# Mixture of experts on one core: experts in the order of their counts, with columns fixed by rank

## The reference, cut to what matters

```python
probs = softmax(xt @ gate_w); top_p, top_i = top_k(probs, 2)      # 8 experts
for k in range(2):
    e, w = top_i[:, k], top_p[:, k]
    pos = position of the token among those whose k-th choice is e
    keep = pos < 160                                              # cap
    buf[e, pos] = xt * keep
    h = gelu(buf @ w1[e] + b1[e])                                 # 256 -> 1024
    y = h @ w2[e] + b2[e] + gelu(buf @ wd[e]) @ wu[e]
    out += y[e, pos] * keep * w
sh = gelu(xt @ sw1 + sb1) @ sw2 + sb2 + gelu(xt @ swd) @ swu
out = x + out + 0.2 * sh
```

## Time and profile before

| | us |
|---|---|
| median of 3 runs | 205.83 (204.18 to 205.94) |
| the profiled execution | 205.79 |
| its span, first to last instruction | 203.8 |
| PE busy | 193.6 (95%) |
| DVE busy | 142.3 (70%) |
| ACT busy | 132.6 (65%) |
| POOL busy | 110.5 (54%) |
| mean granted clock of PE | 0.987 |

### The profile page before, as it was taken

The page is one execution under the profiler, slowest core; times in us unless marked ns, Lnnn a source line. Parts: engine busy times, 40 slices in busy tenths (PEclk is TensorE's granted clock), DMA queues, the critical chain, the costliest instruction groups (busy, mean ns, idle before and its releaser), DMA issues.

```text
span 203.8 us, 4011 instructions
## 1 busy us (share of the span) xinstructions
PE 193.6 (95%) x1457; PEld 185.7 (91%) x1457; DVE 142.3 (70%) x308; ACT 132.6 (65%) x282; POOL 110.5 (54%) x131
## 2 busy tenths in 40 slices
PE   6999999998999999999999999999999999999960
PEld 6987779996789999999999999999999999999950
DVE  4498598859284214777897897888888887988210
ACT  2366899604295109959959959959959959949100
POOL 5400031499570251412896896886886835817471
PEclk9999999999699999999999999999999999999998
DMA  5591845307427022045858858858868765701432
GB/s 164 166 322 53 248 168 157 118 0 228 141 82 222 0 66 103 29 133 178 201 114 275 192 131 259 188 149 263 161 169 252 149 198 184 130 8 15 54 37 34
DMA packets 23816, 29.24 MB, mean 143 GB/s; under 512 B 4442, under 2 KB 20564, under 8 KB 23796
## 3 DMA queue, kind: packets, MB, share of 16 engines
q1 hardware_dynamic: 19412, 23.03, 35.5%
q0 software_dynamic: 4016, 5.38, 16.4%
q10 hardware_dynamic: 368, 0.56, 0.9%
HBM read 23.92 MB, written 5.05 MB: 142 GB/s over the span
## 4 chain that ended last, share of the span: by engine, by line
PE 75%; POOL 8%; DMA 4%; issue 4%; DVE 4%; ACT 1%; POOLq 1%; SPq 0%; DVEq 0%
PE hid_ps L826 12%; PE hid_ps L827 11%; PE hid_ps L828 11%; PE y_ps L828 9%; PE y_ps L826 9%; PE y_ps L827 9%; POOL at_place L398 6%; DMA gate_raw<-in_L_ffn_gate_w 3%; PE turn_ps L991 3%; DMA out_rows<-y_row,slot_tok 2%; POOL out_rows L384 2%; PE row_ps L1007 1%; PE hid_ps L847 1%; DVE gelu_f L601 1%; PE y_ps L953 1%
## 5 line engine op out<-in xcount | busy, mean ns | idle before, releaser
L597 DVE TENSOR_TENSOR hid_l<-gelu_f,hid_h 128x320 fp32r<-128x320 f32 (+1 forms) x80 | 42.0, 533 | 22.3 <-ACT hid_h L504 21.8
L384 POOL DMA_INDIRECT out_rows<-y_row,slot_tok x24 | 43.5, 1813 | 17.3 <-DVE y_row L750 8.9
L503 ACT ACTIVATE gelu_f<-hid_ps,bias_t 128x320 f32<-128x320 f32 (+1 forms) x77 | 44.4, 577 | 9.2 <-PE hid_ps L828 8.7
L504 ACT ACTIVATE hid_h<-hid_ps,bias_t 128x320 fp32r<-128x320 f32 (+1 forms) x77 | 44.6, 580 | 0.0
L370 POOL DMA_INDIRECT slot_in<-slot_rows,slot_src x24 | 26.7, 1111 | 22.7 <-PE turn_ps L991 15.4
L826 PE MATMUL hid_ps<-xs_h,w_h 128*128 128x288 f32 x128 | 38.2, 298 | 0.0
L828 PE MATMUL hid_ps<-xs_h,w_l 128*128 128x288 f32 x128 | 37.7, 294 | 0.0
L827 PE MATMUL hid_ps<-xs_l,w_h 128*128 128x288 f32 x128 | 37.6, 294 | 0.0
L828 PE MATMUL y_ps<-hid_h,w_l 128*128 128x288 f32 x112 | 32.9, 294 | 0.0
L827 PE MATMUL y_ps<-hid_l,w_h 128*128 128x288 f32 x112 | 32.9, 294 | 0.0
L826 PE MATMUL y_ps<-hid_h,w_h 128*128 128x288 f32 x112 | 32.9, 294 | 0.0
(11 more groups left out here) (189 smaller groups left out, 407.8 us busy)
## 6 DMA issues: line engine op xcount, KB each, us to landing
w_raw<-in_L_ffn_w SPq DMA_DIRECT2D x16, 1024.0 KB
x_in<-in_x SPq DMA_DIRECT2D x2, 512.0 KB, 4.5
w_raw<-in_L_ffn_sw SPq DMA_DIRECT2D x1, 1024.0 KB
slot_rows<-token_row SPq DMA_DIRECT2D x2, 512.0 KB, 4.2
out_rows<-base SPq DMA_DIRECT2D x2, 512.0 KB, 3.0
wu_raw<-in_L_ffn_wu SPq DMA_DIRECT2D x24, 32.0 KB
w_raw<-in_L_ffn_sw ACTq DMA_DIRECT2D x1, 512.0 KB
w_raw<-in_L_ffn_sw SPq DMA_DIRECT2D x1, 512.0 KB, 5.3
```

Of the source, the lines that this page charges most:

```text
L384: pool.indirect_dma_start(out=out, out_offset=bass.IndirectOffsetOnAxis(ap=slot_tok[0:n, e, s:s + 1].bitcast(U32), axis=0), in_=y_row[0:n, ...
L503: act.activation(gelu_f[:, j % 3, 0:n], src[:, 0:n], ACT.Gelu, bias=bias(j - 1))
L504: act.activation(hid_h[:, j - 1, 0:n], src[:, 0:n], ACT.Gelu, bias=bias(j - 1)).then_inc(hid_gelu, 1)
L597: dve.tensor_tensor(hid_l[:, j - 1, 0:n], gelu_f[:, j % 3, 0:n], hid_h[:, j - 1, 0:n].bitcast(F32), ALU.subtract).then_inc(hid_split, 1)
```

## The change

- DVE's tables are keyed by an expert's rank (the order of falling used slots, ties by number) instead of its number. So slots, gathers and scatters of "expert r" are those of the r-th fullest.
- The ranks are worked out on POOL (`rank_experts`: 14 small steps that each wait for the one before, then a copy to `order` and two scalings to `steps_down`). The counts come by an ACT copy behind gelu tile 4 of the first half, and `count_before` goes from behind hidden tile 6 to behind tile 4.
- SP reads the expert's number from `order` into a register ahead of each load of weights; the first load of an expert's w1 waits for `order`. DVE sorts the biases by rank (`sort_biases`, two passes over 512 columns).
- PE's sizes are 288, 288, 272, 272, 256, 256, 256, 256 for ranks 0 to 7, if each used count fits; else 320 for all. `turn_slots` turns only the tiles that the next expert's size needs. `last_out` leaves out the third tile when the size is 256, but for one product with 64 rows that fills its bank (POOL and DVE still weigh and scatter it), and the third tile comes first.
- `map_slots` goes from behind hidden tile 1 of the second half to behind tile 5; `side_data` from split 1 to split 5.
- wd and wu of the first expert go on POOL behind at_place, on DVE behind split 6; the first expert's w2 chunks go on DVE behind the shared rows, on ACT behind the gelus of the second half.
- In the last expert `weigh_rows(6)` comes ahead of all splits, and the four w2 chunks come behind splits 1 to 4 (all four, where three came in the period before).
- The scatters have no bounds check.

```diff
+STEP = P // 8
+COUNT_AT = 4
+STEPS_AT = (2, 4)
+SIZES = [FEW - STEP * sum(r >= s for s in STEPS_AT) for r in range(E)]
...
+        last_tiles = [ST - 1] + list(range(ST - 1))
...
             def load_first(v):
-                e = v - 1
+                if v == 1:
+                    sp.wait_ge(order_known, 1)
+                at_rank[v] = sp.value_load(order[0:1, v - 1:v], min_val=0, max_val=E - 1)
+                e = at_rank[v]
                 sp.wait_ge(w1_lo, v * CHUNKS)
...
-                        in_=y_row[0:n, s, :], in_offset=None, bounds_check=T + SLOTS - 1,
+                        in_=y_row[0:n, s, :], in_offset=None,
                         compute_op=ALU.add).then_inc(combined, 16)
...
             wd_hi_part(0, 0)
             wu_hi_part(0, 0)
-            wd_hi_part(1, 1)
-            wu_hi_part(1, 1)
...
+            def rank(ins):
+                ranks[0] += 1
+                ins.then_inc(ranking, 1)
+                pool.wait_ge(ranking, ranks[0])
+
+            def rank_experts():
+                pool.wait_ge(used_copied, 1)
+                pool.wait_ge(consts, 11)
+                rank(pool.tensor_scalar(count16[:, :, :], used_raw[:, :, :], float(CAP), float(E), ALU.min, ALU.mult))
+                rank(pool.tensor_tensor(tie[:, :], count16[:, 0, :], count16[:, 1, :], ALU.add))
+                rank(pool.tensor_tensor(tie[:, :], tie[:, :], col_of[:, 0, :], ALU.subtract))
+                rank(pool.tensor_tensor(is_more[:, :, :], tie[:, :].unsqueeze(1).to_broadcast([P, E, E]),
+                                        tie[:, :].unsqueeze(2).to_broadcast([P, E, E]), ALU.subtract))
...
+                pool.tensor_copy(order[:, :], tie[:, :]).then_inc(order_known, 1)
+                for i, s in enumerate(STEPS_AT):
+                    ins = pool.tensor_scalar(steps_down[:, i, :], rank_at[:, :], float(s), float(STEP), ALU.is_ge, ALU.mult)
+                ins.then_inc(rank_ready, 1)
...
             for j in range(HT):
                 gelu_tile(0, j, HALF, shared_bias)
+                if j == COUNT_AT:
+                    act.wait_ge(pos_made, 1)
+                    act.activation(used_raw[:, :, :], turn_ps[0][:, NT * K * E:(NT + 1) * K * E].rearrange(
+                        "p (k e) -> p k e", k=K), ACT.Copy).then_inc(used_copied, 1)
             for c in range(CHUNKS):
                 w1_chunk(1, 1, c)
+            for j in range(HT):
+                gelu_tile(1, j, HALF, shared_bias)
             for c in range(CHUNKS):
                 w2_chunk(1, 1, c)
-            for j in range(HT):
-                gelu_tile(1, j, HALF, shared_bias)
...
             def key_tokens():
 
+                dve.wait_ge(rank_ready, 1)
+                step(dve.tensor_tensor(picked[:, :, :, :], chosen[:, :, :, :],
+                                       rank_at[:, :].unsqueeze(1).unsqueeze(1).to_broadcast([P, NT, K, E]), ALU.mult))
+                step(dve.tensor_reduce(rank_tok[:, :, :], picked[:, :, :, :], AX_X, ALU.add))
...
-            wd_part(1, 1)
-            wu_part(1, 1)
             for j in range(HT):
                 split_tile(1, j, HALF)
-                if 1 <= j <= CHUNKS:
-                    w2_chunk(j - 1, 1, 1)
-                if j == 1:
+                if j == 5:
                     side_data()
+                if j == 6:
+                    wd_part(1, 1)
+                    wu_part(1, 1)
             for t in range(HTILES, NT):
                 shared_row(t)
+                if t == HTILES:
+                    w2_chunk(0, 1, 1)
+                    w2_chunk(1, 1, 1)
                 if t == HTILES + 1:
                     slots_lo_part(0)
+                if t == HTILES + 2:
+                    sort_biases()
+            w2_chunk(2, 1, 1)
+            w2_chunk(3, 1, 1)
 
             def period(e, par, rows=True, split=True):
 
+                if e == E - 1:
+                    weigh_rows(e - 1, 1 - par)
...
-                    for c in range(CHUNKS - LATE_LO):
+                    for c in range(CHUNKS - LATE_LO if e + 2 < E else 0):
...
-                    if h == 0 and j == HT - 3:
+                    if h == 0 and j == COUNT_AT:
                         count_before()
-                    if h == 1 and j == 1:
+                    if h == 1 and j == 5:
                         map_slots()
...
             with pe.If(most <= FEW):
-                experts(FEW)
+                experts(SIZES)
             with pe.Else():
-                experts(SLOTS)
+                experts([SLOTS] * E)
```

More of the change, by code:

```diff
@@ L189, in build @@
         places_known = sem("places_known")
+        ranking = sem("ranking")
+        used_copied = sem("used_copied")
+        order_known = sem("order_known")
+        rank_ready = sem("rank_ready")
+        bias_picked = sem("bias_picked")
+        bias_sorted = sem("bias_sorted")
         keyed_made = sem("keyed_made")
@@ L711, in value_tokens, with sort_biases @@
                 step(dve.tensor_tensor(used_by[:, :], used[:, 0, :], used[:, 1, :], ALU.add))
+                for i in range(len(STEPS_AT)):
+                    step(dve.tensor_tensor(used_by[:, :], used_by[:, :], steps_down[:, i, :], ALU.add))
                 dve.tensor_reduce(most_used[:, :], used_by[:, :], AX_X, ALU.max).then_inc(used_known, 1)
+            def sort_biases():
+                picks = y_t[:, :, :].rearrange("p k n -> p (k n)")[:, 0:E * NF * E].rearrange("p (r f e) -> p r f e", r=E, f=NF)
+                dve.tensor_tensor(picks, bias_t[:, 0:N_BIAS1].rearrange("p (e f) -> p f e", e=E).unsqueeze(1).to_broadcast(
+                    [P, E, NF, E]), has_rank[:, :, :].unsqueeze(2).to_broadcast([P, E, NF, E]), ALU.mult).then_inc(bias_picked, 1)
+                dve.wait_ge(bias_picked, 1)
+                dve.tensor_reduce(bias_s[:, :, :], picks, AX_X, ALU.add).then_inc(bias_sorted, 1)
             def side_data():
@@ L756, in weigh_last @@
                 dve.wait_ge(slots_sided, 1)
-                for s in range(ST):
+                for i, s in enumerate(last_tiles):
                     n = ST_ROWS[s]
-                    dve.wait_ge(y_made, y_before(e + 2) + (s + 1))
+                    dve.wait_ge(y_made, y_before(e + 2) + (i + 1))
                     dve.tensor_scalar(y_row[0:n, s, :], last_bank[s][0:n, 0:D], slot_w[0:n, e, s:s + 1], None,
@@ L966, in last_out @@
                 pe.wait_ge(y_weighted, e * ST)
-                for s in range(ST):
+                pe.wait_ge(hid_split, hid_count(e + 2, 0))
+                tiles = [s for s in last_tiles if size > s * P]
+                if ST - 1 not in tiles:
+                    pe.matmul(last_bank[ST - 1][0:ST_ROWS[ST - 1], 0:D], low_s[:, (ST - 1) * P:SLOTS], wu_s[par][:, :],
+                              start=True, stop=True).then_inc(y_made, 1)
+                for s in tiles:
                     n = min(P, size - s * P)
@@ L979, in last_out, with turn_slots @@
                     ins.then_inc(y_made, 1)
-            def turn_slots(e, par):
+            def turn_slots(e, par, tiles):
                 pe.wait_ge(slots_in[par], (e // 2 + 1) * 16 * ST)
                 if e == 0:
-                    pe.wait_ge(consts, 9)
+                    pe.wait_ge(consts, 11)
                     pe.wait_ge(slots_sided, 1)
@@ L989, in turn_slots @@
                 for k in range(KD):
-                    for s in range(ST):
+                    for s in range(tiles):
                         ins = pe.transpose(turn_ps[k][:, s * P:(s + 1) * P], slot_in[par][:, s, k * P:(k + 1) * P],
@@ L1036, in _, with experts @@
                     if h == 1 and t == 1:
-                        turn_slots(0, 0)
-            def experts(size):
-                for e in range(E):
+                        turn_slots(0, 0, ST)
+            def experts(sizes):
+                for e, size in enumerate(sizes):
                     other = (e + 1) % 2
@@ L1048, in experts @@
                     if e < E - 1:
-                        turn_slots(e + 1, other)
+                        turn_slots(e + 1, other, (sizes[e + 1] + P - 1) // P)
                         for m in range(KD):
```

62 lines of the change are left out of this document (49 added, 13 removed).

## The result

The median after is 198.57 us (197.73 to 199.96, four runs), against 205.88 us for the kernel before in the same job: a ratio of 0.966, interval 0.960 to 0.973. The change makes the kernel 7.3 us faster; 11.1 us were forecast. 198.57 lies just above the predicted range.

A forecast was written before the change was run, and what follows sets the result against it. PE was taken to bound the expert loop, busy 95% of the span. Shorter experts 5.75, less 0.1 for small waits, map and clock 3.5, end 1.9: 11.05 us off 205.79, giving 194.7 us, range 192.2 to 198.2.

The forecast's parts named there:

- the steps: POOL's rank chain: 0.9 us each for four steps to 34 us, 0.45 after; order at 38.7, no cost forecast.
- The map: PE's map products, moved later in the second half, would take 1.75 us instead of 3.53: 1.8 us saved.
- The clock's part: Eight hidden products behind the map would take 1.8 us instead of 3.5 at full clock: 1.7 us saved.
- SP's reading of the register: SP reading the expert's number ahead of the first w1 load: 0.5 us, between 0 and 1.5.
- the first load: Load of the first expert's w1, issued behind the order: 5.8 us, so the order may come at 39.8.
- It just fits: POOL's loop of about 13.5 us fits PE's 13.6 us period in the short experts; 0.1 us added for small waits.
- rival (b): Short experts: POOL or DVE binds at 14.2 us for a 13.6 period, taking back 2.4 us: 197.1; chance 0.12.
- The pace terms: PE's expert products: 272 columns save 0.0058 us each, 256 save 0.0117; with fewer transposes, 5.75 us before H.
- H: Begin of the last expert's hidden products, 180.1 us in the profile before; times at the end count from it.
- The chain of scatters: POOL's scatters carry the end: third scatter at H+16.25, end at H+21.8 instead of H+23.7, 1.9 us saved.
- The third tile that `last_out` leaves out: Last expert's third output tile, 2.9 us of PE, hidden behind the scatter chain: costs and gives nothing.
- The bounds check: Removing it from scatters saves 0.15 us in each of six on the end's chain, bounds 0 to 0.6.

The follow-up runs named there:

- second set of runs: The changed kernel measured again with no edit, beside other experiments on one chip: 199.07 us, ratio 0.971.
- ACT_W2 = 4: The changed kernel with all four w2 high parts made by ACT from the second expert on, none by POOL: 195.22 us, ratio 0.948.
- old kernel with new sizes: The kernel before with 288, 288, 272, 272, then 256 columns by expert number; tokens in slots past them left out: 205.58 us, ratio 0.996.
- new kernel with old sizes: The changed kernel with 288 columns for every expert, all else of the change kept: 203.09 us, ratio 0.985.
- two-tile kernel: The changed kernel without the third tile's gather, weighing, scatter and bank-filling product for ranks 4 to 7: 194.30 us, ratio 0.945.

## Why the prediction missed

**Front.** Right, but for one execution. The order came at 38.53 and rank_ready at 39.18 (38.7 and 39.3 forecast), though the steps were priced wrong one by one: the first took 2.20 us, the others 0.19 to 0.73. The map cost 1.71 us (1.75) and the clock held. The gain to the first turning was 3.3 us in the second set of runs, 3.2 in the ACT_W2 = 4 kernel, 3.5 forecast. The clock's part of it, some 1.6 us, is not lost in every execution of the old front, as the profile of the old kernel with new sizes shows; the forecast took it as fixed. SP's reading of the register, 0.5 in the forecast and from no row, was 0.97 from the order to the issue of the load (39.50-38.53). The term that varied is the first load, 5.8 us: 5.5 in one execution, 7.7 in another with the same issue time, and there PE stood 1.5 us where the forecast had 0.

**Experts.** The step that failed is the one on POOL, "so its loop needs about 13.5. It just fits", with the 0.1 us for small waits. It took durations from a period of 15.0 us as if they were fixed. With a shorter period POOL's instructions move against DVE's: the third scatter and the small casts fall beside DVE's splits, a cast of w2 holds up a pair of splits by 1.5 us, and the round needs 14.64 us (15.40 the next time). DVE then waits 2.0 us for POOL's cast in each late period, and PE's periods are 14.9 us on average for 13.7. It was rival (b), with its place (POOL, 14.2 us for a period) and its sign right, but with a chance of 0.12 and 2.4 us, where the runs lost 3.6 us (first profile, 102.62 from first to last turning for 99.0) and 2.9 (second, 101.92). The pace terms were right: 272 columns saved 0.0065 us a product ((15.02-14.67)+(15.02-14.35) over 54+104 products, ACT_W2 = 4; 0.0058 taken), and the period for 256 columns is 13.6. That POOL's casts and the length of its round are the cause is shown by two edits that take them away, and by the 288 columns, where the same work waits for nothing. That the durations grow because the instructions meet is read from the timelines.

The Trainium skill (SBUF — State Buffer, "SBUF: two separate sides") has DVE operations with two SBUF inputs and POOL operations that read SBUF exclude each other for whole instructions. The prediction weighed it for the rank chain only, where by that rule the order would have come at about 40.5; it came at 38.53. The late experts are where the trace agrees: 2.79 us for 1.28.

**End.** From the last hidden products (last turning, 0.44 and 6.0 us) to the end were 22.05 us in the ACT_W2 = 4 kernel and 22.15 in the kernel after, 21.8 forecast and 23.7 before; y_row of expert 6 came at H+2.3. But the reason is not quite the forecast's. The chain of scatters was forecast to carry the end with PE's last tile hidden behind it; in the runs PE carries it. The last y_row waits for PE:

```profile
190.70 0.48 DVE L848 TENSOR_SCALAR y_row<-y_ps,slot_w 128x256 f32<-128x256 f32 x1 [2.51 <-PE y_ps L926]
```

That row is at H+14.65 (H+14.3 forecast for the tile). The third tile that `last_out` leaves out was forecast to give nothing. But with 288 columns, where it stays, the same edit of the end loses 0.7 us; so the 1.6 us gained are the third tile's. The bounds check, 0.9 us of the forecast over six scatters, is worth nothing. And two more misses cancel: the last scatter starts at H+15.4 to 15.6 (16.25 forecast), but from its start to the end are 6.7 and 6.5 us (5.6 forecast). That the end came out near its forecast is luck.

**The sum.** Forecast 11.05 us. The ACT_W2 = 4 kernel, where POOL is out of the way, is 206.23-195.22 = 11.0 us faster than the old kernel of its job. So the account of the path was right in sum (the end's terms in part by luck, as above). What the kernel after lacks, 11.0 for its own 7.3 and 5.9 us in two jobs, some 4 to 5 us, came back when POOL's casts went to ACT. By parts, each against the old kernel of its job: new kernel with old sizes 3.1 us; with the sizes on top 5.9 to 7.3; and 11.0 with POOL relieved. What stays open: whether in ACT_W2 = 4 it is the shorter round or the missing meetings of POOL's casts with DVE that helps. The two-tile kernel shows that a shorter round gives most of it, the kernel with wd and wu loaded first shows that a round with room does not help while a cast stands beside DVE's work for PE. And in the old kernel with new sizes it is open what the slower nine executions lost beyond the end.

## What to carry to other kernels

When the bounding engine's work in a loop is cut, compare the new period with the whole round of each other engine, waits and issue gaps included, and allow for durations that grow when instructions of two engines meet: here a round that should use 13.5 of 13.6 us didn't fit. Then ask which meetings lie on the bounding engine's path. A scatter of 4.17 us off the path cost nothing, a cast beside three small splits on it went with 0.7 us lost a period. Take the work off the engine that has no slack first, here by giving ACT, with time to spare, the casts that POOL made. And price an edit of the end against every engine's path, not only against the one that now comes last.

## What the runs showed of the hardware

- A pair of DVE subtractions with two SBUF inputs took 1.28 us with no GpSimd cast beside it (at 129.55 a scatter stood beside it), 1.77 beside a cast that took 2.13 (kernel before, 117.34), and 2.79 beside one that took 1.68 (kernel after, 115.20).
- GpSimd's scatters took 1.42 to 1.57 us when quiet. In the profiles of the kernels before, after and with ACT_W2 = 4, all that took over 2.6 us (up to 4.17) stood beside DVE's splits, but others beside splits took no longer than quiet ones (1.44 at 174.78, kernel after). A gather took 3.09 us beside splits (ACT_W2 = 4, 129.24) and 0.95 when quiet.
- After an idle stretch of 12.5 us, the first small GpSimd step (16 columns) took 2.20 us, the dependent ones after it 0.19 to 0.73 with 0.07 to 0.09 between. Whether the idle time, the operation or DVE's work beside it makes the first long wasn't tried. POOL's timeline:

```profile
30.30 2.20 POOL L436 TENSOR_SCALAR count<-used_raw 128x16 f32<-128x16 f32 x1 [12.52 <-ACT used_raw L581]
32.58 0.73 POOL L437 TENSOR_TENSOR tie<-count 128x8 f32<-128x8 f32 x1
```

- Sixteen products of 72 columns (1.71 us) in a full PE left the clock at 1.00, where the same products with waits, 3.3 to 3.5 us long, were followed by 0.66 in one profile (kernel before, 51 to 56 us) and by 1.00 in another (old kernel with new sizes).
- The same 1 MB load, issued at the same time, was read after 5.5 us in one execution and after 7.7 in another.
